# An attention's 32 divisions moved from VectorE to GpSimd, in a kernel written engine by engine for one core

## The reference

```python
h = tokenizer(x)                                   # 64 blocks of 5 tokens of 256
h = concatenate([h, txt], axis=1)                  # 64 x 82 x 256
h = h + attention(layernorm(h))
h = h + experts(layernorm(h))

# attention, 16 heads of 16
scores = einsum('bhqd,bhkd->bhqk', q, k) * scale + bias
attn = softmax(scores)
out = einsum('bhqk,bhkd->bhqd', attn, v)           # the division can be done after this product
return out @ w_out + b_out
```

## Time and profile before

| | us |
|---|---|
| median of 3 runs | 612.51 (611.25 to 613.08) |
| the profiled execution | 612.77 |
| its span on the core | 610.9 |
| PE busy | 549.6 (90%) |
| VectorE busy | 476.8 (78%) |
| ScalarE busy | 367.2 (60%) |
| GpSimd busy | 314.5 (51%) |

### The profile page before, as it was taken

How to read it: one execution, slowest core, us unless ns; L and a number is a source line. 1 busy time by engine, 2 the same in 40 slices (tenths; PEclk the granted TensorE clock), 3 DMA queues, 4 the chain that set the end, 5 groups by cost and what they waited for, 6 DMA issues and landing times.

```text
span 610.9 us, 20474 instructions
## 1 busy us (share of the span) xinstructions
PE 549.6 (90%) x7904; PEld 460.2 (75%) x7904; DVE 476.8 (78%) x967; ACT 367.2 (60%) x793; POOL 314.5 (51%) x401
## 2 busy tenths in 40 slices
PE   8999989889999999989998999999897779999940
PEld 7788867667787778767787888887776668888830
DVE  3666868999989999998998988998866645666617
ACT  1222234257766777767776776776666647777724
POOL 1577772637558688888886434441211233444430
PEclk9999999999999999999999999999998989999975
DMA  8999103223333245567656433433433454545339
GB/s 292 396 332 335 47 9 104 89 76 99 92 96 92 94 136 181 157 188 233 190 170 215 158 121 109 129 91 110 127 108 98 91 117 107 106 114 114 80 131 323
DMA packets 79722, 89.51 MB, mean 147 GB/s; under 512 B 35086, under 2 KB 60174, under 8 KB 79116
## 3 DMA queue, kind: packets, MB, share of 16 engines
q1 hardware_dynamic: 74876, 78.20, 42.1%
q0 software_dynamic: 4464, 9.35, 4.9%
q10 hardware_dynamic: 288, 0.66, 0.3%
HBM read 48.82 MB, written 36.29 MB: 139 GB/s over the span
## 4 chain that ended last, share of the span: by engine, by line
PE 56%; DVE 22%; issue 11%; DMA 4%; ACT 3%; SPq 2%; DVEq 1%; POOL 1%; POOLq 0%; ACTq 0%
PE banks L1452 7%; DVE mx L1846 7%; PE banks L1418 6%; PE banks L1562 6%; PE banks L1577 5%; PE banks L283 5%; PE banks L1464 4%; PE banks L1476 4%; PE banks L1430 4%; DVE prob L1848 3%; PE banks L1443 3%; DVE qk_space L1834 3%; PE banks L323 2%; PE banks L1547 2%; PE banks L331 2%
## 5 line engine op out<-in xcount | busy, mean ns | idle before, releaser
L1685 ACT ACTIVATE probT<-banks 82x328 f32<-82x328 f32 x256 | 109.3, 435 | 9.7 <-PE banks L1452 9.6
L1452 PE MATMUL banks<-ident_all,prob 82*82 82x82 f32 x1024 | 110.4, 239 | 1.5 <-ACT early L1665 1.5
L1846 DVE TENSOR_REDUCE mx<-banks 82x8 f32<-82x656 f32 x128 | 104.2, 814 | 8.1 <-PE banks L1443 7.3
L1848 DVE TENSOR_TENSOR prob<-banks,mx 82x656 f32<-82x656 f32 x128 | 107.1, 836 | 4.4
L1452 PEld LDWEIGHTS banks<-ident_all,prob 82*82 82x82 f32 x1024 | 88.7, 121 | 28.9 <-issue 7.5
L1677 ACT ACTIVATE prob<-prob 82x656 f32<-82x656 f32 x128 | 95.5, 746 | 15.0 <-DVE prob L1848 13.9
L1296 POOL TENSOR_TENSOR big<-big,gwq 128x256 f32<-128x256 f32 x41 | 29.9, 730 | 100.4 <-ACT gwq L1672 99.9
L1418 PE MATMUL banks<-hT,wqkv 128*128 128x328 f32 (+10 forms) x320 | 80.5, 386 | 0.0
L1357 POOL DMA_INDIRECT entry_rows<-cwT,slot_entry x39 | 39.7, 1019 | 66.0 <-ACT cwT L1730 60.2
L1665 ACT ACTIVATE early<-banks 128x328 f32<-128x328 f32 x64 | 28.5, 445 | 67.8 <-PE banks L1464 55.5
L1464 PE MATMUL banks<-probT,vv 82*32 82x82 f32 x2048 | 50.1, 238 | 18.2 <-ACT probT L1685 9.2
(11 more groups left out here) (275 smaller groups left out, 1013.9 us busy)
## 6 DMA issues: line engine op xcount, KB each, us to landing
vv<-value_rows SPq DMA_DIRECT2D x57, 192.0 KB
value_rows<-vs SPq DMA_DIRECT2D x41, 256.0 KB, 2.3
share<-shares SPq DMA_DIRECT2D x32, 164.0 KB
slot_rows<-xh SPq DMA_DIRECT2D x1, 4992.0 KB, 32.9
fused_rows<-in_txt SPq DMA_DIRECT2D x1, 4928.0 KB, 20.4
big<-in_patches SPq DMA_DIRECT2D x2, 1600.0 KB, 12.3
out<-big SPq DMA_DIRECT2D x25, 128.0 KB, 2.0
big<-entry_rows SPq DMA_DIRECT2D x6, 512.0 KB, 6.5
```

The source lines that it names most:

```text
L1452: mm = te.transpose(bank(("turn", 4 * b + g))[0:T, s * T:s * T + T], prob[:, b % 2, g, s, :], ident_all[0:T, 0:T])
L1685: act.activation(probT[:, b % 2, g, :, :].rearrange("p s t -> p (s t)"), bank(("turn", 4 * b + g))[0:T, 0:4 * T], ACT.Copy).then_inc(S["pr ...
L1846: v.tensor_reduce(mx[:, half, :, :], s4, X, ALU.max).then_inc(S["max_ready"], 1)
L1848: v.tensor_tensor(prob[:, b % 2, 2 * half:2 * half + 2, :, :], s4, mx[:, half, :, :].unsqueeze(3).to_broadcast([T, 2, 4, T]), ALU.subtract ...
```

## The change

`divide` goes from VectorE's program to GpSimd's, with its waits, its operands and its semaphore as they were; only the engine's name changes in it. On GpSimd division m stands ahead of `add_project` in the iteration 2m + 6, division 30 ahead of the first scatter, and division 31 behind the two scatters of the first pair.

```diff
@@ gpsimd
+        def divide(m):
+
+            pool.wait_ge(S["share_in"], 16 * (m + 1))
+            pool.wait_ge(S["packed%d" % (m % 2)], 64 * (m // 2 + 1))
+            done = (2 * T * m + 2 * T - RA + 127) // 128
+            if done > 0:
+                pool.wait_ge(S["project_done"], done)
+            both = sums[:, m % 2, 0:2, :, :].rearrange("p c n t -> p c (n t)")
+            for a, lo, size in pieces(2 * T * m, 2 * T, RA):
+                ins = pool.tensor_tensor(attT[:, :, a:a + size], both[:, :, lo:lo + size], share[:, :, lo:lo + size], ALU.mult)
+            ins.then_inc(S["attT_ready"], 1)
...
+            if b >= 6 and b % 2 == 0:
+                divide(b // 2 - 3)
             for n in projected(b - 1):
                 add_project(n)
...
         for n in range(NTL - 3, NTL):
             add_row(n)
+        divide(NB // 2 - 2)
         for p in range(NPAIR):
             for h in halves(p):
                 scatter(2 * p + h)
+            if p == 0:
+                divide(NB // 2 - 1)
             if p < 2:
                 add_project(NTL - 4 + 2 * p)
                 add_project(NTL - 3 + 2 * p)
@@ vector
-            if b >= 5 and b % 2 == 1:
-                divide(b // 2 - 2)
         own_wb(0, owners[0])
...
         own_wb(1, owners[1])
-        divide(NB // 2 - 2)
         copy_t2(0)
...
             copy_t2(p)
-            if p == 1:
-                divide(NB // 2 - 1)
```

More of the change, by code:

```diff
@@ L1863, in invert @@
             v.reciprocal(den[:], den[:]).then_inc(S["rden_ready"], 1)
[L1865 to L1875, removed]
         def experts(p):
```

## The result

The changed kernel took 620.55 us (median, 618.38 to 623.33) against 611.88 us for the kernel before: 8.7 us or 1.4% slower by the medians. The ratio, which is computed apart from the medians, is 1.0201 with a 95% interval of 1.0135 to 1.0268, that is 8.3 to 16.4 us. A second comparison, with more runs, gave a ratio of 1.0156 (1.0103 to 1.0208), and 8.6 us by the medians. The forecast was 616.8 us, 4.3 us slower, in a range of 609 to 623.5: the direction and the range held, the loss was twice the size. The profiled execution took 620.36 us with a span of 618.5, 7.6 us more than the span before.

A forecast was written before the change was run, and what follows sets the result against it. It took TensorE, busy 90% of the span, as the bound. Against 612.77 us profiled, +10 + 2 - 0.7 - 1 - 1 - 5 = +4.3 gave 617.1, as a median 616.8 us, range 609 to 623.5.

The forecast's parts named there:

- the seam's -5 us: Where attention ends and expert pairs begin (475 to 505 us): VectorE freed, PE idle and slow clock gone, 5 us saved.
- +10 + 2 - 0.7 - 1 - 1 = +9.3: Late divisions +10, clock +2, POOL's shorter rows -0.7, PE idle before 204 us -1 and after 330 us -1.
- The division's price: On POOL, one division of 328 elements takes 0.95 us, or 1.1 us where the ring's end splits it.
- The late divisions: From 204 to 330 us, POOL reaches divisions 7, 11 and 14 late; ScalarE's copy and PE wait, 10 us lost.
- no wait worth naming from 222 to 325 us: Sign of a right forecast: in the dense stretch's profile after, POOL shows no wait worth naming.
- The clock: Behind the idles at divisions 7 and 14 PE runs mostly at 1.2 GHz: 2 us lost, bounds 0 and 4.5.
- VectorE's copies of expert weights come 1 us sooner, so PE's 1.07 us before 480.89 goes: In the seam, division 29 done on POOL about 475 us frees VectorE, so PE's 1.07 us idle goes.
- Division 31: In the seam, it no longer holds back pair 3's weights: PE's first product 3.5 us sooner, 5 us with clock.
- Before 204 us: Ahead of the dense stretch, removing divisions from VectorE saves 1 us of PE's 2.6 us of idle.
- Behind 330 us: From 330 to 475 us, removing divisions from VectorE saves 1 us of PE idle.
- the third, 622 us: Rival, chance 0.18: slow clock at each stall costs 4.5 us, last shares land late, seam gives only 2; +10 us.

The follow-up runs named there:

- e2_loop_only: Against the kernel before, only divisions 0 to 28 on GpSimd, the last three on VectorE: 621.19 us, ratio 1.0154.
- e1_seam_only: Against the kernel before, only divisions 29, 30 and 31 on GpSimd, 0 to 28 on VectorE: 607.95 us against 611.33, ratio 0.9952.
- g3: The changed kernel once more, all divisions on GpSimd, on another comparison's chip: 618.22 us, ratio 1.0156 to the kernel before.
- g2: The changed kernel with GpSimd's row additions 33 to 40 moved to iterations 58 to 63: 618.15 us, ratio 1.0146 to the kernel before.
- f2: The kernel before, all divisions on VectorE, plus 27 division-sized GpSimd products that nobody awaits: 612.87 us against 609.61, ratio 1.0049.
- g1: Against the kernel before, only divisions 7, 11 and 14 on GpSimd, the other 29 on VectorE: 618.86 us against 609.62, ratio 1.0145.

## Why the prediction was right in its direction and half in its size

The step that failed is the seam's -5 us. The other terms, +10 + 2 - 0.7 - 1 - 1 = +9.3, are the loop's, and the loop alone lost 9.4 us (e2_loop_only). The seam alone gave 2.9 (e1_seam_only), and beside the moved loop nothing that the times show. 9.4 - 2.9 is 6.5, and the two kernels' medians give the same sum, where the whole change lost 8.6 and 8.7 by the medians; the 2 us between them lie inside the intervals, and their cause stays open. That the loop's sum came out is in part luck, as its terms were off to both sides.

- **The division's price** held: 0.89 us (estimate 0.95), and 1.02 for two parts (1.1). The line between the two rows had 0.885; the 0.07 us for taking up after a wait is shown by no run. Here is its line, after, as in the earlier trace rows; 0.88 us median on POOL against 0.49 on VectorE:

```profile
L1327 POOL TENSOR_TENSOR wkv<-early,share x42: 203/876/1054, 149.3 to 507.6; 128x328 f32<-128x328 f32 x22, 128x40 f32<-128x40 f32 x1, 128x288 f32<-128x288 f32 x1, 128x80 f32<-128x80 f32 x1
```

- **The late divisions** held. The forecast had them late by 4.9, 2.1 and 5.8 us; the copies' shift rose by 5.1 (from -1.56 to +3.55), 3.2 (+3.11 to +6.29) and 5.6 (+4.32 to +9.88). PE stood 4.25, 2.26 and 4.72 us. Divisions 10 and 12, which the forecast had in time, were late by 1.8 and 1.9 us, and PE stood another 1.17 and 0.70. I had POOL with no wait worth naming from 222 to 325 us. That was wrong: it waited 2.63 us at 239.32 and 3.03 at 326.5 for ScalarE, since a late division holds back the projection that POOL's next addition needs.
- **The clock** fell further than forecast ("I take 2 us, with 0 and 4.5 as bounds"), but what it took from PE is not what it cost in time. The busy time in short stretches, after, with the granted clock behind POOL's column:

```profile
230.00:236.00 6.00, 2.43 (x51) 1.71 (x42) 4.20 (x8) 0.12 (x1) 5.48 (x8) 1.00 0.48 155
236.00:243.00 7.00, 6.30 (x88) 5.41 (x88) 1.52 (x5) 4.71 (x11) 3.43 (x7) 0.76 0.41 131
...
284.00:290.00 6.00, 4.02 (x85) 3.23 (x86) 3.50 (x9) 4.29 (x11) 4.83 (x8) 1.00 0.48 158
...
322.00:331.00 9.00, 7.56 (x90) 6.49 (x91) 1.77 (x3) 4.86 (x12) 4.48 (x7) 0.62 0.26 87
```

  The kernel before, in two of these stretches:

```profile
236.00:243.00 7.00, 6.95 (x140) 5.93 (x143) 6.19 (x13) 5.43 (x13) 6.10 (x10) 1.00 0.61 195
322.00:331.00 9.00, 7.20 (x164) 5.95 (x162) 8.59 (x16) 5.43 (x14) 6.54 (x9) 1.00 0.63 203
```

  Behind PE's idles of 4.25 and 4.72 us PE ran in part at 1.2 GHz: 0.24 x 7 + 0.38 x 9 = 5.1 us taken from it, above the bound. Behind the idle of 2.26 us the clock stayed at 1.00. What this costs in time can be read from four traces whose dense stretch has the same program: the changed kernel twice (the second is g3), e2 and g2. In e2 and g2 the clock fell behind division 11 too; e2:

```profile
284.00:290.00 6.00, 3.37 (x39) 2.81 (x31) 3.75 (x7) 2.06 (x6) 5.51 (x8) 0.82 0.71 220
290.00:300.00 10.00, 10.00 (x164) 7.65 (x163) 7.22 (x15) 6.27 (x14) 6.92 (x10) 0.77 0.54 167
```

  By the same sum over all three stalls (236 to 250, 284 to 300 and 322 to 340 us) the clock took 10.2 us from PE in e2 and g2, and 5.1 in the changed kernel both times. Yet the step of the table from copy 13 to copy 34 is 14.7 and 14.6 us there, and 13.0 and 13.2 here: 5.1 us more of slow clock cost 1.5 us more time. So most of it was covered, as the forecast had supposed, even though POOL too waited for PE's projections. How the 13.0 us divide between clock and lateness is not shown; nothing here shows that 2 us were too few for the clock.
- **The seam** was the mis-sized term. It gave 3.8 us of the forecast 5 in this pair of traces: 2.5 on the way from pair 2 to pair 3 and 1.7 from pair 3 to pair 4, less 0.4 in front of them. Its step "VectorE's copies of expert weights come 1 us sooner, so PE's 1.07 us before 480.89 goes" failed: the additions and the copies fell upon each other, and PE stood 2.38 us. Division 31 no longer keeps pair 3's weights back, and PE comes to it without a stop, as forecast. But the forecast took the idle of 2.46 us ahead of pair 3, and the 1.7 us of slow clock behind it, for the kernel's own. Some 1.1 us of the one and all of the other are this one execution's: in the three other kernels whose seam divisions are VectorE's (e2, f2, g1) PE stood 1.19, 1.41 and 1.41 us there, and the clock behind it was 1.00; PE's first product of pair 3 and the stretch behind it, in e2:

```profile
510.88 0.66 PE L1566 MATMUL banks<-pc,qk_space 128*64 128x128 f32 x8 [1.19 <-issue]
```

```profile
511.00:513.50 2.50, 2.50 (x41) 2.33 (x41) 2.13 (x5) 1.83 (x3) 0.88 (x1) 1.00 0.52 134
```

  From pair 3 to pair 4 the kernel before took 8.35 us and these three 6.7. From pair 0 to pair 5 the four took 35.0, 33.7, 31.6 and 30.5 us (before, g1, e2, f2), the ten others 29.1 to 31.7. By their means (32.7 and 30.3) the seam gives 2.4 us, and by the kernel that moved only these three, 2.9 us; the trace I had was the longest of the four.
- **Before 204 us** held (-1.6 for -1). **Behind 330 us** the forecast's 1 us was 2.0 without the vanished idle. The +2.0 from 440 to 475 us is this execution's, as said under the table.

The rival that came closest was the third, 622 us. Its 2 us for the seam are near the 2.9 measured, but not for its reason, as no late share made PE wait there. A slow clock at each stall is seen in e2 and g2, and at two of the three stalls in the changed kernel; that it cost 4.5 us, as this rival has it, is not shown.

## What to carry to other kernels

Before work goes to an engine that looks idle on the page, set the engine's place in its own program beside the moment at which each result is asked for, in the stretch where it is busiest; here 3 of 32 places decided, and leaving those divisions (or the eleven of the dense stretch) with VectorE turned a loss of 1.4 to 2.0% into a gain of 0.7 to 1.0%. Where a place is late, putting the work earlier in that engine's order removes most of the loss without moving it back. Before a wait or a slow stretch of one trace goes into a sum as a gain, look for it in a second execution: 2.8 of the forecast's 5 us, a part of an idle and the slow clock behind it, stood in one trace out of four. And a slow clock's loss is not its cost: here 1.5 of 5.1 us showed in the time.

## What the runs showed of the hardware

- VectorE's copies of 64 x 640 f32 took 0.50 us alone and 0.85 to 1.0 us beside GpSimd's additions of 128 x 256 f32, which went from 0.73 to 0.94 us: two engines that don't wait for each other's data slowed each other, and moving the additions gave the 0.50 back.
- The clock fell behind PE's idles of 4.25 and 4.72 us (0.76 over 7 us, 0.62 over 9 us) and not behind one of 2.26 us. With the three divisions alone on POOL it was 0.69 and 0.62 in the same two stretches, behind idles of 2.83 us. The idle's length alone does not tell: behind division 11 the clock fell after 2.35 and 2.63 us (g2, e2: 0.83 and 0.82 from 284 to 290 us) and stayed at 1.00 after 2.26 and 2.84 (the changed kernel, twice).
